# Cross attention: thirteen probability transposes in one run, score steps in runs of 4 and 12, value tiles in blocks of 7 and 6

## The chip, the cores and the metric

One core of one Trainium2 chip runs the whole program. The metric is device time in microseconds (us) for one launch. The time before is the median of three runs.

## The reference, cut to what matters

The program computes one block of a perceiver: cross attention of 32 sequences of 64 rows over a context of 1601 rows each (width 512), then causal self attention with 16 heads, then a two-stage mixture of 64 experts. The change touches cross attention alone:

```python
q = einsum('bsd,ed->bse', layernorm(x), Wq) + bq      # x:   32 x 64 x 512
k = einsum('btd,ed->bte', ctx, Wk) + bk               # ctx: 32 x 1601 x 512
v = einsum('btd,ed->bte', ctx, Wv) + bv
scores = einsum('bse,bte->bst', q, k)
attended = einsum('bst,bte->bse', softmax(scores), v)
x = x + attended
```

The kernel folds `Wq` and `Wk` into one product ahead of time and applies `Wv` after the attention, so that the large loop multiplies queries and probabilities with the raw context.

## The kernel before, in words

**Pairs.** Cross attention works on 16 pairs of sequences (`PAIRS`), so that 2 x 64 query rows fill 128 partitions. For each pair p there are four kinds of work on TensorE:

- `score(pe, p, db)`, 16 steps (`STEPS_S`). Each step multiplies 32 of the 512 features. It needs the context transposed for that step, which VectorE writes into `z`, a ring of 4 slots (`RING`): `blocks` (line 549) makes two transposes for each step, of 7 and of 6 context tiles. VectorE may write a slot again when the score step that read it has finished (line 548). The scores of a pair build up in PSUM banks 0 to 3. A step is 8 calls of `matmul` (line 537), which the trace shows as 16 instructions.
- `transpose_prob(p, g)`, for g = 0 to 3: 4, 4, 4 and 1 transposes of the probabilities (line 676) into PSUM. ScalarE copies each group to `probt` in SBUF (lines 658 and 661).
- `attend(p, j)`, 13 value tiles (`TILES`), each of 4 instructions in the trace (line 686), added up in PSUM bank 6 (`OB`). Each releases part of the context buffer through `s_pv`.
- `transpose_attended(p)`: 4 transposes of the attended rows (line 695) into bank 7 (`AB`).

**Order on TensorE.** The order is written out by hand and shifted by one pair. Iteration p (1 to 15) runs score steps of pair p. Among them it runs the probability transposes of pair p-1, one group ahead of each of the steps 0 to 3, then value tiles 0 to 3 ahead of step 4 and tiles 4 to 6 ahead of step 8. After step 15 come tiles 7 to 12, and then `transpose_attended(p - 2)`. In runs, the score steps are 1, 1, 1, 1, 4 and 8.

**PSUM.** The probability transposes use banks 4 and 5 in turn (`TB + g % 2`), so from the third group on TensorE waits for ScalarE's copy of the group before last (`s_pte`). Value tile j waits for the copy that holds it.

**Between score step 15 and the next transposes.** VectorE takes the maximum of each row (`greatest`, lines 555 to 561), ScalarE then computes the exponentials (`exponentials`, lines 570 to 574, six semaphore increments of `s_exp`), and the first probability transpose of the pair waits for all six. ScalarE's order in an iteration is: `exponentials(p)`, `attended_out(p - 2)` (copies the transposed attended rows out of bank 7, line 644), `attended(p - 1)` (normalises bank 6 into `att`, line 638), four copies of probabilities.

**Loads.** The context lies in 5 slots, two for a pair (7 and 6 tiles). SyncE's queue loads a slot again in two parts, after value tiles 4 and 7 for the slot of the first 7 tiles and after tiles 11 and 13 for the other (lines 597 and 185). It also stores the attended rows (`store_attended`, line 585) and reloads the queries (line 195). The store of pair p-2 stands ahead of the query load in its order.

**The two ends.** Before iteration 1 a preparation stage ends with a small copy on ScalarE (line 408, semaphore `s_re`). TensorE waits for it in iteration 1 after score step 0. After iteration 15 TensorE transposes the last probabilities, does 8 value projections (`values`, line 234, 16 instructions), and then the last pair's 13 value tiles.

Of the kernel before, what the change touches and what calls it, by code (L numbers as in the profile page):

```python
# [27 lines left out]
P = 128  # L28
# [3 lines left out]
QUADS = SEQS // 4  # L32
# [7 lines left out]
FULL = CTX // P  # L40
REST = CTX - FULL * P
RQ = REST // 4
TILES = FULL + 1
# [114 lines left out]
PAIRS = SEQS // 2  # L158
# [73 lines left out]
def values(pe, ps, early, par, c):  # L232

    x = pe.matmul(ps[:, par, :], early.ats[:, c, par::2], early.xwv[:, c, :], start=c == 0, stop=c == DC - 1)  # L234
    if c == DC - 1:
        x.then_inc(early.s_p1, 1)
# [266 lines left out]
def cross(nc, block, sem, zone, area, spare, temp, ps, a, ident, qbias, halves, slots, qs, s_c, s_qs, s_qd, early):  # L503
# [4 lines left out]
    prob = zone(TILES, 4, 32)  # L508
    probt = zone(TILES, P)
# [5 lines left out]
    RAT = FULL * 32  # L515
    WIDTH = (RAT + RQ + 1, RAT + RQ, RAT + RQ, RAT + RQ)
    EXPS = 6
    TB, OB, AB = 4, 6, 7

    s_pad = sem("cr_pad")  # L520
    s_z, s_s, s_pv = sem("cr_z"), sem("cr_s"), early.s_pv
    s_mx, s_top, s_bias = sem("cr_mx"), sem("cr_top"), sem("cr_bias")
    s_exp, s_tot, s_rec = sem("cr_exp"), sem("cr_tot"), sem("cr_rec")
    s_pt, s_pte = sem("cr_pt"), sem("cr_pte")
    s_att, s_at, s_ate = sem("cr_att"), sem("cr_at"), sem("cr_ate")
# [5 lines left out]
    def score(pe, p, db):  # L531
        at = STEPS_S * p + db
        pe.wait_ge(s_z, 2 * at + 2)
        for tb in range(4):
            r = slice(tb * 32, (tb + 1) * 32)
            for b in range(2):
                last = pe.matmul(ps[b * SEQ:(b + 1) * SEQ, tb, 0:WIDTH[tb]],  # L537
                                 qs[p % 2][r, db, b * SEQ:(b + 1) * SEQ], z[r, at % RING, b, 0:WIDTH[tb]],
                                 start=db == 0, stop=db == STEPS_S - 1)
        last.then_inc(s_s, 1)  # L540
# [23 lines left out]
    def exponentials(act, p):  # L564
        act.wait_ge(s_bias, p + 1)
        if p:
            act.wait_ge(s_tot, p)
            act.wait_ge(s_pt, 4 * p)
        for tb in range(4):
            act.activation(prob[:, 0:FULL, tb, :], ps[:, tb, 0:RAT].rearrange("p (j t) -> p j t", t=32), ACT.Exp,  # L570
                           bias=bias[:, 0:1], accum_out=sums[:, tb:tb + 1]).then_inc(s_exp, 1)
        act.activation(prob[:, FULL, :, 0:RQ], ps[:, 0:4, RAT:RAT + RQ], ACT.Exp,
                       bias=bias[:, 0:1], accum_out=sums[:, 4:5]).then_inc(s_exp, 1)
        act.activation(prob[:, FULL, 0, RQ:RQ + 1], ps[:, 0, RAT + RQ:RAT + RQ + 1], ACT.Exp,
                       bias=bias[:, 0:1], accum_out=sums[:, 5:6]).then_inc(s_exp, 1)

    s_re = prepare(nc, block, sem, area, spare, temp, ps, a, ident, qbias, halves, slots, qs, s_c, s_qs, s_qd,
                   s_pad, prob[:, FULL, :, :],
                   {"score": score, "blocks": blocks, "greatest": greatest, "exponentials": exponentials})

    @block.sync
    def _(sp):
        def store_attended(p):
            sp.wait_ge(s_ate, p + 1)
            sp.dma_start(a["at"][p // 2, :, :, p % 2 * P:(p % 2 + 1) * P], att_t).then_inc(s_atd, 16)

        for p in range(PAIRS):
            if p >= 2:
                store_attended(p - 2)
            if p + 2 < PAIRS:  # L590
                sp.wait_ge(s_s, STEPS_S * (p + 1))
                sp.wait_ge(s_qd, 8 * 16 * ((p + 2) // 2 + 1))
                load_queries(sp, a, qs, s_qs, p + 2)
            for k, first in ((2 * p + 5, 0), (2 * p + 6, 7)):
                for part in range(2):
                    if k < 2 * PAIRS:
                        sp.wait_ge(s_pv, TILES * p + min(first + (4, 7)[part], TILES))
                        load_context(sp, a, slots, s_c, k, parts=(part,))
            if p == PAIRS - 3:
                early.load(sp, a)  # L600
                sp.wait_ge(s_pv, TILES * (PAIRS - 2))
                for n in ("swq", "swk", "swv"):
                    sp.dma_start(early.weights[n], a[n].rearrange("(c p) e -> p c e", p=P)).then_inc(early.s_w, 16)
            if p == PAIRS - 2:
                sp.wait_ge(s_pv, TILES * (PAIRS - 2) + 7)
                sp.dma_start(early.weights["swo"], a["swo"].rearrange("(c p) e -> p c e", p=P)).then_inc(early.s_w, 16)
        sp.wait_ge(s_pv, TILES * (PAIRS - 1))
        early.load_own(sp, a)
        store_attended(PAIRS - 2)
        store_attended(PAIRS - 1)  # L610
# [20 lines left out]
    @block.scalar  # L631
    def _(act):
        def attended(p):
            act.wait_ge(s_pv, TILES * (p + 1))
            act.wait_ge(s_rec, p + 1)
            if p:
                act.wait_ge(s_at, p)
            act.activation(att, ps[:, OB, :], ACT.Copy, scale=recip[:, 0:1]).then_inc(s_att, 1)

        def attended_out(p):  # L640
            act.wait_ge(s_at, p + 1)
            if p:
                act.wait_ge(s_atd, 16 * p)
            act.copy(att_t, ps[:, AB, :].rearrange("p (c n) -> p c n", c=DC)).then_inc(s_ate, 1)

        for p in range(PAIRS):
            if p:
                exponentials(act, p)
            if p >= 2:
                attended_out(p - 2)  # L650
            if p:
                attended(p - 1)
            for g in range(4):
                act.wait_ge(s_pt, 4 * p + g + 1)
                if p and g == 0:
                    act.wait_ge(s_pv, TILES * p)
                if g < 3:
                    act.copy(probt[:, 4 * g:4 * g + 4, :], ps[:, TB + g % 2, :].rearrange("p (j n) -> p j n", j=4))\
                       .then_inc(s_pte, 1)
                else:  # L660
                    act.copy(probt[:, FULL, :], ps[:, TB + 1, 0:P]).then_inc(s_pte, 1)
        attended_out(PAIRS - 2)
        attended(PAIRS - 1)
        attended_out(PAIRS - 1)

    @block.tensor
    def _(pe):
        def transpose_prob(p, g):
            if g == 0:
                pe.wait_ge(s_exp, EXPS * (p + 1))  # L670
            n = 4 * p + g
            if n >= 2:
                pe.wait_ge(s_pte, n - 1)
            for j in quarter(g):
                at = (j - 4 * g) * P
                last = pe.transpose(ps[:, TB + g % 2, at:at + P], prob[:, j, :, :].rearrange("p b t -> p (b t)"), ident)  # L676
            last.then_inc(s_pt, 1)

        def attend(p, j):
            if j % 4 == 0:  # L680
                pe.wait_ge(s_pte, 4 * p + j // 4 + 1)
            if j == 0 and p:
                pe.wait_ge(s_att, p)
            slot, jj = (slots[slot_of(2 * p)], j) if j < 7 else (slots[slot_of(2 * p + 1)], j - 7)
            for b in range(2):
                last = pe.matmul(ps[b * SEQ:(b + 1) * SEQ, OB, :], probt[:, j, b * SEQ:(b + 1) * SEQ],  # L686
                                 slot[:, b, jj, :], start=j == 0, stop=j == TILES - 1)
            last.then_inc(s_pv, 1)

        def transpose_attended(p):  # L690
            pe.wait_ge(s_att, p + 1)
            if p:
                pe.wait_ge(s_ate, p)
            for c in range(DC):
                last = pe.transpose(ps[:, AB, c * P:(c + 1) * P], att[:, c * P:(c + 1) * P], ident)
            last.then_inc(s_at, 1)

        for p in range(1, PAIRS):
            pe.wait_ge(s_qs[p % 2], 64 * (p // 2 + 1))
            for db in range(STEPS_S):  # L700
                if p == 1 and db == 1:
                    pe.wait_ge(s_re, 2 * QUADS)
                if db < 4:
                    transpose_prob(p - 1, db)
                if db in (4, 8):
                    for j in ((0, 1, 2, 3) if db == 4 else (4, 5, 6)):
                        attend(p - 1, j)
                score(pe, p, db)
            for j in range(7, TILES):
                attend(p - 1, j)  # L710
            if p >= 2:
                transpose_attended(p - 2)
        for g in range(4):
            transpose_prob(PAIRS - 1, g)
        pe.wait_ge(early.s_xwv, 16)
        pe.wait_ge(early.s_ats, 16)
        for par in range(2):
            for c in range(DC):
                values(pe, ps, early, par, c)
        transpose_attended(PAIRS - 2)  # L720
        for j in range(TILES):
            attend(PAIRS - 1, j)
        transpose_attended(PAIRS - 1)

# [1585 lines left out]
```

## Time and profile before

| what | value |
|---|---|
| median of 3 runs | 1348.16 us (1347.85 to 1349.36) |
| profiled execution, span from first to last instruction | 1344.9 us |
| granted TensorE clock, mean over the span | 0.969 |
| TensorE matmul busy | 1251.8 us, 93% of the span |
| VectorE busy | 797.4 us, 59% |
| ScalarE busy | 439.9 us, 33% |
| period of one pair in cross attention | 26.42 us |

The page's shares are means over three stages with different limits. The change acts only between about 121 us and 540 us of the span. The profile gives no separate launch-to-end time of the profiled execution. Its span lies 3.3 us below the median of the runs, and that part is outside the first and last instruction.

### The profile page before, as it was taken

What the parts mean: (1) busy time and instruction counts of PE and PEld (TensorE: products, weight loads), DVE (VectorE), ACT (ScalarE), POOL (GpSimd) and SP (SyncE); (2) the same over time, 40 slices, a digit from 0 to 9 for tenths busy, and PEclk for the clock granted to TensorE, in tenths of its full rate; (3) what the DMA queues carried; (4) which work ended last, traced back from release to release, by engine and by line L of the source; (5) the groups of instructions that cost most, each with busy time, mean ns of one, the idle gap of its engine ahead of it and who ended that gap; (6) DMA issues with size and microseconds to landing.
All of it is one profiled execution on the core that took longest, in us unless ns stands there. A gap on an engine that the chain in (4) does not pass through costs nothing.

```text
span 1344.9 us, 61468 instructions
## 1 busy us (share of the span) xinstructions
PE 1251.8 (93%) x27944; PEld 813.3 (60%) x27944; DVE 797.4 (59%) x1489; ACT 439.9 (33%) x873; POOL 226.4 (17%) x372
## 2 busy tenths in 40 slices
PE   6999999999999999999999999787898888889886
PEld 4875333333333333676667665666787777779775
DVE  2264777677677763355655655454665746465766
ACT  0332132113112211221222212234554646454564
POOL 0000000000000001121222212114351533212212
PEclk9999999999999999999999999897999998995998
DMA  6686889998998992611011110401311206334012
GB/s 262 203 284 167 294 273 318 293 304 292 313 291 285 316 325 87 113 63 43 19 62 62 62 47 17 109 33 64 125 79 77 117 8 238 134 164 179 28 44 94
DMA packets 68083, 211.52 MB, mean 157 GB/s; under 512 B 14449, under 2 KB 30833, under 8 KB 53521
## 3 DMA queue, kind: packets, MB, share of 16 engines
q1 hardware_dynamic: 67984, 210.16, 46.1%
q8 instruction: 69, 1.13, 0.3%
q14 instruction: 30, 0.24, 0.1%
HBM read 172.37 MB, written 37.75 MB: 156 GB/s over the span
## 4 chain that ended last, share of the span: by engine, by line
PE 77%; DVE 10%; issue 5%; DMA 3%; POOL 2%; ACT 1%; SPq 1%; DVEq 0%; POOLq 0%; ACTq 0%
PE ps L686 14%; PE ps L537 10%; PE ps L1059 8%; PE ps L2142 6%; DVE arena L549 5%; PE ps L2093 4%; PE ps L234 4%; PE ps L1173 4%; PE ps L1080 4%; PE ps L444 3%; PE ps L2071 2%; PE ps L2184 2%; PE ps L676 2%; DVE arena L1823 2%; PE ps L2128 2%
## 5 line engine op out<-in xcount | busy, mean ns | idle before, releaser
L549 DVE STREAM_TRANSPOSE arena<-arena 128x448 f32<-128x448 f32 (+1 forms) x512 | 264.2, 578 | 103.2 <-PE ps L537 85.9
L537 PE MATMUL ps<-arena 32*64 32x400 f32 (+1 forms) x4096 | 202.6, 506 | 0.8
L686 PE MATMUL ps<-arena 128*64 128x512 f32 x832 | 189.1, 598 | 0.0
L537 PEld LDWEIGHTS ps<-arena 32*64 32x64 f32 x4096 | 75.1, 130 | 97.5 <-issue 49.8
L686 PEld LDWEIGHTS ps<-arena 128*64 128x64 f32 x832 | 55.6, 136 | 121.3 <-issue 111.9
L570 ACT ACTIVATE arena<-ps,arena 128x384 f32<-128x384 f32 x64 | 36.3, 581 | 276.4 <-DVE arena L561 276.4
L1059 PE MATMUL ps<-arena 128*128 128x256 f32 x512 | 116.2, 385 | 0.8 <-ACT arena L994 0.8
L1059 PEld LDWEIGHTS ps<-arena 128*128 128x128 f32 x512 | 97.9, 193 | 17.8 <-issue 3.3
L1993 ACT COPY arena<-ps 128x512 f32<-128x512 f32 x128 | 74.9, 586 | 84.5 <-PE ps L2142 58.0
L1823 DVE SCALAR_TENSOR_TENSOR arena<-ps,arena 128x512 f32<-128x512 f32 x64 | 69.9, 1118 | 43.6 <-PE ps L2128 43.3
L2142 PE MATMUL ps<-arena 64*64 64x32 f32 x4096 | 84.1, 236 | 4.3 <-issue 4.0
L859 POOL TENSOR_TENSOR arena<-arena 128x1024 f32<-128x1024 f32 x8 | 18.9, 2368 | 406.5 <-PE ps L686 406.5
L2142 PEld LDWEIGHTS ps<-arena 64*64 64x64 f32 x4096 | 78.0, 153 | 8.2 <-issue 5.3
L2093 PE MATMUL ps<-arena 64*32 64x128 f32 x4096 | 70.3, 277 | 12.2 <-issue 6.3
L2093 PEld LDWEIGHTS ps<-arena 64*32 64x32 f32 x4096 | 59.6, 107 | 23.3 <-issue 18.9
L927 DVE SCALAR_TENSOR_TENSOR arena<-ps,arena 128x512 f32<-128x512 f32 x32 | 20.6, 686 | 81.6 <-PE ps L1070 81.6
L1762 POOL COPY arena<-arena 128x512 f32<-128x512 f32 x64 | 41.7, 656 | 160.8 <-ACT arena L2014 89.0
L2168 PE MATMUL ps<-arena 64*64 64x256 f32 x1024 | 62.0, 394 | 6.1 <-DVE arena L1836 3.5
L234 PE MATMUL ps<-arena 128*128 128x512 f32 x128 | 60.2, 605 | 0.0
L1814 DVE COPY arena<-ps 128x512 f32<-128x512 f32 x64 | 43.6, 687 | 27.5 <-PE ps L2093 27.4
L1080 PE MATMUL ps<-arena 128*64 128x256 f32 x512 | 58.8, 380 | 0.0
L877 POOL TENSOR_TENSOR arena<-arena 128x512 f32<-128x512 f32 x32 | 33.4, 1042 | 150.0 <-DVE arena L944 150.0
(146 smaller groups left out, 1844.4 us busy)
## 6 DMA issues: line engine op xcount, KB each, us to landing
arena<-ctx SPq DMA_DIRECT2D x64, 1024.0 KB
arena<-ctx SPq DMA_DIRECT2D x32, 768.0 KB
arena<-q_n SPq DMA_DIRECT2D x64, 256.0 KB, 11.3
h_n<-arena SPq DMA_DIRECT2D x16, 1024.0 KB, 4.4
arena<-h_n SPq DMA_DIRECT2D x16, 1024.0 KB, 9.3
arena<-x SPq DMA_DIRECT2D x16, 512.0 KB, 4.7
arena<-ctx SPq DMA_DIRECT2D x32, 256.0 KB
x_n<-arena SPq DMA_DIRECT2D x16, 512.0 KB, 3.5
```

What stands on the lines that cost most here:

```text
L234: x = pe.matmul(ps[:, par, :], early.ats[:, c, par::2], early.xwv[:, c, :], start=c == 0, stop=c == DC - 1)
L537: last = pe.matmul(ps[b * SEQ:(b + 1) * SEQ, tb, 0:WIDTH[tb]], qs[p % 2][r, db, b * SEQ:(b + 1) * SEQ], z[r, at % RING, b, 0:WIDTH[tb]], s ...
L549: vec.transpose(z[:, at % RING, :, g * 224:g * 224 + nt * 32].rearrange("p b (j t) -> p b j t", t=32), slots[slot_of(k)][:, :, 0:nt, db * ...
L686: last = pe.matmul(ps[b * SEQ:(b + 1) * SEQ, OB, :], probt[:, j, b * SEQ:(b + 1) * SEQ], slot[:, b, jj, :], start=j == 0, stop=j == TILES - 1)
L1059: last = pe.matmul(ps[:, bank, m % 2 * QROWS:(m % 2 + 1) * QROWS], w[n][:, c, m * P:(m + 1) * P], lnt[:, c, :], start=c == 0, stop=c == DC ...
L1080: last = pe.matmul(ps[e * SEQ:(e + 1) * SEQ, 2 + pair, s2 * 256:(s2 + 1) * 256], lnt[:, c, at:at + SEQ], w["swv"][:, c, :].rearrange("p (m ...
L1173: last = pe.matmul(ps[:, (OUT if more else LAST_OUT) + par, :], aot[:, c, par::2], w["swo"][:, c, :], start=c == 0, stop=c == DC - 1)
L1823: vec.scalar_tensor_tensor(h[:, q, :, at].rearrange("p j g -> p g j"), ps[:, b:b + 2, :].rearrange("p b (g x) -> p (b g) x", x=2 * F1)[:, ...
L1993: act.copy(mid[u].rearrange("p (b x) -> p b x", b=2), ps[:, 2 * u:2 * u + 2, 0:256]).then_inc(s_me, 1)
L2093: last = pe.matmul(ps[c * R:(c + 1) * R, 4 * v + hf, o * P:(o + 1) * P], tab_st[v][r, o, :], x, start=True, stop=True)
L2142: last = pe.matmul(ps[k * F1:(k + 1) * F1, 2 * u + t, g * D1:(g + 1) * D1], st_h[u][rows_t, g * F1:(g + 1) * F1], two(st_a[u])[rows_t, k, ...
L2168: last = pe.matmul(ps[t * E:(t + 1) * E, 2 * (g % 4) + hf, o % 2 * 2 * P:(o % 2 + 1) * 2 * P], tab_dn[v][r, o, :], x, start=True, stop=True)
```

## The change

What it does, part by part:

- The probability transposes of a pair run one after another at the head of an iteration and write four banks: 4, 5, 7 and 6. They no longer wait for ScalarE's copies. Groups 2 and 3 wait instead until banks 7 and 6 have been read (`s_ate`, `s_att`).
- The score steps then run as 0 to 3 and 4 to 15. Between them stand value tiles 0 to 6 and `transpose_attended(p - 2)`. Tiles 7 to 12 stay after step 15.
- The first value tile waits for all four copies of the probabilities.
- In ScalarE's order `attended_out` moves behind the four copies and one pair earlier in index (p-1 in iteration p).
- The wait on `s_re` in iteration 1 moves ahead of the transposes.
- At the end `transpose_attended(PAIRS - 2)` moves from ahead of the last value tiles to between tiles 6 and 7.

```diff
-    TB, OB, AB = 4, 6, 7
+    OB, AB = 6, 7
+    PROB_BANKS = (4, 5, AB, OB)
...
             if p:
                 exponentials(act, p)
-            if p >= 2:
-                attended_out(p - 2)
             if p:
                 attended(p - 1)
             for g in range(4):
                 act.wait_ge(s_pt, 4 * p + g + 1)
-                if p and g == 0:
-                    act.wait_ge(s_pv, TILES * p)
+                bank = PROB_BANKS[g]
...
-        attended_out(PAIRS - 2)
+            if p:
+                attended_out(p - 1)
         attended(PAIRS - 1)
         attended_out(PAIRS - 1)
...
-            n = 4 * p + g
-            if n >= 2:
-                pe.wait_ge(s_pte, n - 1)
+            if PROB_BANKS[g] == AB and p >= 2:
+                pe.wait_ge(s_ate, p - 1)
+            if PROB_BANKS[g] == OB and p:
+                pe.wait_ge(s_att, p)
...
         def attend(p, j):
-            if j % 4 == 0:
-                pe.wait_ge(s_pte, 4 * p + j // 4 + 1)
-            if j == 0 and p:
-                pe.wait_ge(s_att, p)
+            if j == 0:
+                pe.wait_ge(s_pte, 4 * p + 4)
...
         for p in range(1, PAIRS):
             pe.wait_ge(s_qs[p % 2], 64 * (p // 2 + 1))
+            if p == 1:
+                pe.wait_ge(s_re, 2 * QUADS)
+            for g in range(4):
+                transpose_prob(p - 1, g)
             for db in range(STEPS_S):
-                if p == 1 and db == 1:
-                    pe.wait_ge(s_re, 2 * QUADS)
-                if db < 4:
-                    transpose_prob(p - 1, db)
-                if db in (4, 8):
-                    for j in ((0, 1, 2, 3) if db == 4 else (4, 5, 6)):
+                if db == 4:
+                    for j in range(7):
                         attend(p - 1, j)
+                    if p >= 2:
+                        transpose_attended(p - 2)
                 score(pe, p, db)
             for j in range(7, TILES):
                 attend(p - 1, j)
-            if p >= 2:
-                transpose_attended(p - 2)
...
+        for j in range(7):
+            attend(PAIRS - 1, j)
         transpose_attended(PAIRS - 2)
-        for j in range(TILES):
+        for j in range(7, TILES):
             attend(PAIRS - 1, j)
         transpose_attended(PAIRS - 1)
```

## Rows read from the trace of the kernel before

**Rows 1.** Timeline of TensorE, one pair (start us, us, instruction, count).

```profile
305.43 0.66 PE L695 MATMUL ps<-arena 128*128 128x128 f32 x4
305.92 0.60 PE L676 MATMUL ps<-arena 128*128 128x128 f32 x4
306.45 0.93 PE L537 MATMUL ps<-arena 32*64 32x401 f32 x16
...
311.32 3.66 PE L686 MATMUL ps<-arena 128*64 128x512 f32 x16
314.91 2.94 PE L537 MATMUL ps<-arena 32*64 32x401 f32 x64
317.78 2.80 PE L686 MATMUL ps<-arena 128*64 128x512 f32 x12
320.51 6.09 PE L537 MATMUL ps<-arena 32*64 32x401 f32 x128
326.53 5.38 PE L686 MATMUL ps<-arena 128*64 128x512 f32 x24
331.85 0.66 PE L695 MATMUL ps<-arena 128*128 128x128 f32 x4
332.34 0.60 PE L676 MATMUL ps<-arena 128*128 128x128 f32 x4
```

**Rows 2.** Timeline of TensorE, line 695, iterations 2 and 15 (12 lie between).

```profile
173.32 0.66 PE L695 MATMUL ps<-arena 128*128 128x128 f32 x4
...
516.83 0.66 PE L695 MATMUL ps<-arena 128*128 128x128 f32 x4
```

**Rows 3.** Timeline of VectorE and weight loads in the run of eight steps.

```profile
321.55 4.06 DVE L549 STREAM_TRANSPOSE arena<-arena 128x448 f32<-128x448 f32 x8 [1.54 <-PE ps L537]
...
325.67 0.24 PEld L537 LDWEIGHTS ps<-arena 32*64 32x64 f32 x16 [0.75 <-DVE arena L549]
```

**Rows 4.** Timeline from score step 15 to the next transposes, iteration 1 to 2.

```profile
141.64 5.38 PE L686 MATMUL ps<-arena 128*64 128x512 f32 x24
...
147.04 0.23 ACT L574 ACTIVATION_READ_ACCUMULATOR arena<-ps,arena 128x1 f32 x1
147.13 0.71 ACT L638 ACTIVATE arena<-ps,arena 128x512 f32<-128x512 f32 x1
...
147.37 0.63 PE L676 MATMUL ps<-arena 128*128 128x128 f32 x4 [0.35 <-issue]
...
148.03 0.59 ACT L658 COPY arena<-ps 128x512 f32<-128x512 f32 x1 [0.19 <-PE ps L676]
```

**Rows 5.** Timeline, start of iteration 1.

```profile
121.00 0.64 PE L676 MATMUL ps<-arena 128*128 128x128 f32 x4
121.55 0.26 ACT L408 ACTIVATE arena<-ps,arena 128x2 f32<-128x2 f32 x1
```

**Rows 6.** Timeline, end of iteration 15.

```profile
517.32 1.04 PE L676 MATMUL ps<-arena 128*128 128x128 f32 x8
...
519.88 7.04 PE L234 MATMUL ps<-arena 128*128 128x512 f32 x16
```

**Rows 7.** Waits of VectorE, 120 to 540 us (total, times, longest).

```profile
DVE arena L549 <- PE ps L537: 78.9, 47, 3.6
DVE arena L549 <- DMA arena<-ctx: 17.0, 13, 2.4
```

**Rows 8.** Loads: timeline of one pair; DMA issues by line (last number: median us to landing).

```profile
323.55 3.07 SPq L189 DMA_DIRECT2D arena<-ctx  x5
...
at_n<-arena SPq DMA_DIRECT2D x16, 256.0 KB, 10.7
```

**Rows 9.** Windows: length, busy us (count) of PE, PEld, DVE, ACT, POOL; clock, DMA share, GB/s.

```profile
320.50:326.53 6.03, 5.98 (x130) 2.46 (x128) 4.06 (x8) 0.00 (x0) 0.00 (x0) 1.00 0.99 374
...
910.00:915.00 5.00, 1.92 (x9) 1.95 (x10) 0.00 (x0) 0.00 (x0) 0.00 (x0) 0.57 0.01 3
915.00:920.00 5.00, 5.00 (x25) 5.00 (x24) 0.00 (x0) 0.00 (x0) 0.00 (x0) 0.50 0.02 3
```

More of the change, by code:

```diff
@@ L654, in _ @@
                 act.wait_ge(s_pt, 4 * p + g + 1)
-                if p and g == 0:
-                    act.wait_ge(s_pv, TILES * p)
+                bank = PROB_BANKS[g]
                 if g < 3:
-                    act.copy(probt[:, 4 * g:4 * g + 4, :], ps[:, TB + g % 2, :].rearrange("p (j n) -> p j n", j=4))\
+                    act.copy(probt[:, 4 * g:4 * g + 4, :], ps[:, bank, :].rearrange("p (j n) -> p j n", j=4))\
                        .then_inc(s_pte, 1)
                 else:
-                    act.copy(probt[:, FULL, :], ps[:, TB + 1, 0:P]).then_inc(s_pte, 1)
-        attended_out(PAIRS - 2)
+                    act.copy(probt[:, FULL, :], ps[:, bank, 0:P]).then_inc(s_pte, 1)
+            if p:
+                attended_out(p - 1)
         attended(PAIRS - 1)
@@ L670, in transpose_prob @@
                 pe.wait_ge(s_exp, EXPS * (p + 1))
-            n = 4 * p + g
-            if n >= 2:
-                pe.wait_ge(s_pte, n - 1)
+            if PROB_BANKS[g] == AB and p >= 2:
+                pe.wait_ge(s_ate, p - 1)
+            if PROB_BANKS[g] == OB and p:
+                pe.wait_ge(s_att, p)
             for j in quarter(g):
                 at = (j - 4 * g) * P
-                last = pe.transpose(ps[:, TB + g % 2, at:at + P], prob[:, j, :, :].rearrange("p b t -> p (b t)"), ident)
+                last = pe.transpose(ps[:, PROB_BANKS[g], at:at + P], prob[:, j, :, :].rearrange("p b t -> p (b t)"), ident)
             last.then_inc(s_pt, 1)
         def attend(p, j):
-            if j % 4 == 0:
-                pe.wait_ge(s_pte, 4 * p + j // 4 + 1)
-            if j == 0 and p:
-                pe.wait_ge(s_att, p)
+            if j == 0:
+                pe.wait_ge(s_pte, 4 * p + 4)
             slot, jj = (slots[slot_of(2 * p)], j) if j < 7 else (slots[slot_of(2 * p + 1)], j - 7)
```

## The prediction

> **What bounds the kernel now.** I read the page first, then the timeline of TensorE over two pairs, then the same stretch with VectorE, ScalarE and the load queue, then the waits. The page gives TensorE 93% matmul busy, but its matmuls are pipelined, so I go by start-to-start times. In cross attention the groups of TensorE follow one another and the pair repeats: 305.92 to 332.34 is 26.42 us [rows 1], and the thirteen periods from 173.32 to 516.83 give 26.42 each [rows 2]. Four score steps in a run take 314.91 to 317.78, 2.87 us. Eight take 320.51 to 326.53, 6.02 us [rows 1]. Two runs of four would be 5.74. The difference is the first thing to see: the ring holds four steps, and beyond that VectorE sets the pace. It starts 1.04 us after the run does, does 8 transposes in 4.06 us (0.508 each, 1.015 a step), and TensorE's last step follows at 325.67, 0.06 us after VectorE's end [rows 3]. So the chain here is TensorE, then VectorE, then TensorE.
>
> The second thing is the boundary. Score step 15 ends and the tiles start at 326.53. The tiles last until 331.85, and the next probability transposes start at 332.34, 5.81 us after 326.53 [rows 1]. Between iterations 1 and 2, where no `transpose_attended` fills the gap, they start at 147.37, 5.73 us after 141.64, right behind the last exponential (147.27) and not at the tiles' end (141.64 + 5.32 = 146.96) [rows 4]. So the row maxima and the exponentials set this start, and `transpose_attended` lies in a gap of 0.41 us that TensorE has anyway.
>
> **The change part by part.** I write T for the start of the tiles behind score step 15, and add up one iteration from T to the next T. The prices are start-to-start times that hold the cost of going to the next kind.
>
> *Boundary.* Nothing on the chain from VectorE through ScalarE moves ahead of the exponentials. The transposes start at T + 5.73 as in iteration 2 [rows 4]. Before it was 5.81, so 0.08 is gained.
>
> *Thirteen transposes in a run.* Eight in a run take 1.04 where four take 0.60, so one more is 0.11 [rows 1, 6]. Four up to the next score step are 0.53, so thirteen are 0.53 + 9 x 0.11 = 1.52. Then four steps, 2.87. Together 4.39. Before, the same work took 305.92 to 311.32, 5.40 [rows 1]. This gains 1.01: changes of kind fall away, and ScalarE's copies no longer stand between. The copies must be done before tile 0, at T + 5.73 + 4.39 = T + 10.1. ScalarE normalises first (0.71 from 147.13, so until T + 6.2), waits for the first group (T + 5.73 + 0.66) and then makes four copies of 0.59 at most [rows 1, 4], up to T + 8.8. The cover is the four score steps, with 1.3 us to spare; without them tile 0 would stand 1 to 2.4 us later. Group 3 writes bank 6 at T + 7.05 (12 x 0.11 on), after that normalisation, so its new wait costs nothing. Bank 7 is read out in the middle of the iteration before and costs nothing either.
>
> *Ring.* VectorE makes steps 0 to 3 from T + 2.6 on (reductions first) and is done before T + 9.2 even with its longest wait for a load, 2.4 us [rows 7]. Steps 4 to 7 are made under the tiles. The ring is full when the long run starts.
>
> *Seven tiles.* 16 instructions take 3.59, 12 take 2.73 [rows 1], and one change of kind (0.15: 3.59 less 16 x 0.215, the 0.215 from the difference of the two) falls away: 3.59 + 2.73 - 0.15 = 6.17. This gains 0.15.
>
> *`transpose_attended`.* In the middle of the iteration it covers no gap. It costs what four transposes up to a score step cost, 0.53 [rows 1]. This is the only place where its cost becomes visible.
>
> *Twelve steps.* Four are in the ring, and eight are left for VectorE: 1.04 + 16 x 0.508 + 0.06 + the last step up to T (325.67 to 326.53, 0.86) = 10.08 [rows 1, 3]. Before, runs of 4 and 8 took 2.87 + 6.02 = 8.89, since VectorE refilled the ring under tiles 4 to 6. This loses 1.19. If the last ring slots were free sooner it could not help: TensorE never has a step ready in this run that VectorE has not just made. The lower bound is a run paced by TensorE alone: three runs of four less two changes of kind, 3 x 2.87 - 2 x 0.15 = 8.3. I take the 10.08, since the rows show that pace.
>
> *Sum.* 5.73 + 1.52 + 2.87 + 6.17 + 0.53 + 10.08 = 26.90, against 26.42: +0.48 in each of 14 iterations (2 to 15), +6.7. The check by differences: -0.08 - 1.01 - 0.15 + 0.53 + 1.19 = +0.48.
>
> *Iteration 1.* The wait for `s_re` now stands ahead of the transposes. ScalarE's copy ends at 121.81 [rows 5], so they start near 121.95 instead of 121.00: +0.95. The shorter first part gives back 1.01. There is no `transpose_attended`, so tiles and long run make 1.19 - 0.15 = +1.04. Together +1.0.
>
> *End.* After iteration 15 the transposes start 0.08 earlier and take 1.52 where 517.32 to 519.88, 2.56, were spent with two waits for copies [rows 6]: -1.1. The four attended transposes only change place there.
>
> *Loads and queue.* On SyncE's queue the store no longer waits for ScalarE, and the query loads behind it go out some 0.5 us sooner. The second part of the g = 1 slot is now asked for at T - 10.6, before at T - 6; its last requests ended at 326.62 [rows 8]. VectorE's waits for loads (17.0 us in 13 pairs [rows 7]) should shrink or vanish, but they were under the tiles, so I count nothing. ScalarE's `attended_out` now waits for a store asked for at about T + 6, which lands 10.7 later [rows 8], at T + 17, about when its input is ready. Behind it stand the next exponentials, needed at T + 29. Slack 11, cost nothing.
>
> Total: +1.0 + 6.7 - 1.1 = +6.6. On the profiled span 1344.9 to 1351.5. With the 3.3 that lies outside it, and no change to the later stages except the shift, 1348.2 + 6.6 = **1354.8 us**.
>
> **Rivals.**
> *A. The long run is not paced by VectorE* (ends faster). Then twelve steps are 8.3, the pair 25.12, and 15 pairs gain 1.3 each, the ends nothing: about 1329. For it: VectorE idles 78.9 us on TensorE in this stage [rows 7], so in total it has time. Against: those waits come when the ring is full, and 325.67 stands 0.06 behind VectorE in every period. It decides from the point where VectorE's share of the run is 0.48 us shorter, that is 0.06 of 1.015 in each of 8 steps. Chance 0.05.
>
> *B. The pieces cancel* (no measurable change). It needs 0.3 us a pair that I do not see, say a score run that restarts sooner behind `transpose_attended`, or thirteen transposes that overlap the steps. Time 1346 to 1350.8. Chance 0.10.
>
> *C. A new wait in the middle*: copies late for tile 0, or loads in one burst that reach VectorE late. With 1 us a pair: 1354.8 + 15 = 1370. For it: the margin of the copies is only 1.3. Against: each of its parts has a row. Chance 0.06.
>
> *D. TensorE's clock falls in the paced run.* In the run of eight, with the last steps paced by VectorE, the granted clock is 1.00, the level of 2.4 GHz. At 915 to 920 us, after 5 us in which TensorE was busy for 1.92, it is 0.50, that of 1.2 GHz [rows 9]. In the new run TensorE waits about 0.33 us a step (1.015 less 8.3 / 12). At the lower level the run would be 16.6, +6.5 us a pair: 1452. Chance 0.02. The Trainium skill, "TensorE: Matmul & The Clock Gate", section "A second HAM failure mode: psum-queue depth-cycling", says that a kernel which cycles through PSUM banks and leaves small idle gaps between groups of matmuls can swing between the two clock levels; this would speak against four banks and a paced run. By that rule the time would be rival D's. The trace does not agree so far: the paced part it has runs at 1.00.
>
> **How the numbers follow.** My own case, slower by 6.6, has 0.77. Its bounds: the boundary 5.73 or 5.81 (1.1 us over 14), the transposes 1.43 to 1.60 (2.5 us; 13 x 0.11, or 0.60 + 9 x 0.11), attended transposes 0.44 (4 x 0.11) to 0.60 (2.2 us), the later stages 1 us. This makes 1352 to 1358. A change under 0.2% (2.7 us) cannot be told from none. For 8 in 10 I take 1351 to 1359, which reaches a little toward B and C. Faster 0.06 (A and the far end of B), same 0.10, slower 0.84.
>
> **What would show it.** In the new timeline: thirteen transposes of line 676 in about 1.5 us with no ScalarE wait among them, 4.4 us from their start to tile 0; 28 tile instructions in 6.2; line 695 behind them; then 192 score instructions in 10.1 with VectorE unbroken over 16 transposes, ending just ahead of the last step; and T to first transpose 5.7. The distance of two starts of line 695 should be 26.9. I am wrong if the long run takes under 9.5, if the distance is 26.4 or less, or if a wait stands ahead of tile 0.

## The result, and where the time went

The changed kernel takes 1383.73 us (median, 1376.12 to 1389.08, 4 runs) against 1348.01: a ratio of 1.0262, with a 95% interval of 1.0232 to 1.0291. That is slower, as forecast, but by 35.7 us where 6.6 were forecast, and outside the range. The profiled execution has a span of 1387.2 us against 1344.9, 42.3 more; it was the slowest of the four (1389.08 us), so its surplus is larger than that of the medians. Here 1.9 us lie outside the first and last instruction, so the 3.3 us of the section on the time before were only in part that; the rest is scatter between executions. The ratios here leave out runs more than 1.5% above the fastest of their kernel, which are one run of the kernel before, of 6326.19 us and unexplained, and four of the ten of e11.

First the part that was changed. One pair on TensorE in the timeline of the changed kernel (columns as in [rows 1]):

```profile
305.96 5.38 PE L684 MATMUL ps<-arena 128*64 128x512 f32 x24
311.73 1.61 PE L676 MATMUL ps<-arena 128*128 128x128 f32 x13 [0.39 <-ACT arena L575]
313.27 2.94 PE L538 MATMUL ps<-arena 32*64 32x401 f32 x64
316.14 6.25 PE L684 MATMUL ps<-arena 128*64 128x512 f32 x28
322.31 0.66 PE L693 MATMUL ps<-arena 128*128 128x128 f32 x4
322.90 10.03 PE L538 MATMUL ps<-arena 32*64 32x401 f32 x192
332.86 5.38 PE L684 MATMUL ps<-arena 128*64 128x512 f32 x24
```

Start to start these are 5.77, 1.54, 2.87, 6.17, 0.59 and 9.96, together 26.90. The prediction had 5.73, 1.52, 2.87, 6.17, 0.53 and 10.08, together 26.90. VectorE in the long run, and ScalarE ahead of tile 0 of the next pair:

```profile
323.94 8.01 DVE L550 STREAM_TRANSPOSE arena<-arena 128x448 f32<-128x448 f32 x16 [5.32 <-PE ps L538]
```

```profile
338.35 0.71 ACT L639 ACTIVATE arena<-ps,arena 128x512 f32<-128x512 f32 x1
339.30 1.56 ACT L656 COPY arena<-ps 128x512 f32<-128x512 f32 x3 [0.23 <-PE ps L676]
340.73 0.30 ACT L659 COPY arena<-ps 128x128 f32<-128x128 f32 x1
```

Sixteen transposes without a break, starting 1.04 us behind the run and ending at 331.95, 0.91 ahead of the next tiles: VectorE paces the run, as in [rows 3]. The copies end at 341.03, and tile 0 of that pair starts at 343.05.

The head and the end of cross attention:

```profile
122.69 0.51 PE L459 MATMUL ps<-arena 128*128 128x1 f32 x4
123.98 1.61 PE L676 MATMUL ps<-arena 128*128 128x128 f32 x13 [0.78 <-issue]
...
527.56 1.64 PE L676 MATMUL ps<-arena 128*128 128x128 f32 x13 [0.29 <-ACT arena L575]
529.04 7.04 PE L234 MATMUL ps<-arena 128*128 128x512 f32 x16
```

Line 234 starts at 529.04, 9.2 us later than in [rows 6]. Of these 2.0 were lost ahead of the changed code: the last matmul of line 459 starts at 122.9, before at 120.9. (Over the kernels below it starts anywhere from 119.9 to 126.7, so that is scatter.) The changed part itself costs 7.1 up to here. Behind it, up to the first start of line 1050, the order with `transpose_attended` between the last tiles costs 0.3 more (550.15 - 529.04 = 21.11 where 540.66 - 519.88 = 20.78 was).

The rest is far away from the change. I take the down steps of the mixture from the first to the last start of line 2184 (`second_dn`), a line that is the same in both. Before they ran from 1155.4 to 1334.8, 179.4 us; now from 1162.9 to 1377.0, 214.1 us. So they start 7.5 later (the stages between had given 1.7 of the 9.2 back) and take 34.7 more, and with 0.1 behind them that is the whole 42.3. Windows over this stretch (columns as in [rows 9]), of the kernel before:

```profile
1155.00:1209.00 54.00, 45.52 (x1929) 40.12 (x1931) 32.24 (x57) 25.91 (x40) 11.73 (x18) 0.97 0.44 177
1209.00:1249.00 40.00, 38.95 (x1464) 35.69 (x1460) 17.65 (x32) 16.92 (x30) 10.78 (x18) 0.53 0.41 158
1249.00:1335.00 86.00, 74.32 (x3552) 64.74 (x3544) 62.40 (x85) 52.62 (x81) 23.26 (x34) 1.00 0.13 49
```

and of the changed kernel:

```profile
1163.00:1223.00 60.00, 46.54 (x1934) 40.66 (x1932) 32.37 (x57) 27.44 (x42) 12.40 (x19) 0.97 0.41 160
1223.00:1267.00 44.00, 38.03 (x1420) 35.20 (x1422) 17.62 (x31) 14.42 (x26) 10.08 (x16) 0.50 0.37 145
1267.00:1333.00 66.00, 56.56 (x2168) 47.16 (x2160) 45.27 (x55) 39.29 (x56) 13.89 (x20) 0.98 0.09 33
1333.00:1377.00 44.00, 36.66 (x1405) 34.36 (x1408) 17.35 (x30) 14.42 (x26) 8.59 (x14) 0.52 0.13 49
```

Before, one window of 40 us has a granted clock near 0.5 (the level of 1.2 GHz, not 2.4). Now there are two of 44. The timeline shows what TensorE did just ahead of the first of them:

```profile
1215.38 1.10 PE L2168 MATMUL ps<-arena 64*64 64x256 f32 x16
1216.27 1.11 PE L2142 MATMUL ps<-arena 64*64 64x32 f32 x64
1222.85 0.29 PE L2184 MATMUL ps<-arena 128*32 128x32 f32 x2 [5.46 <-issue]
1225.22 0.65 PE L2184 MATMUL ps<-arena 128*32 128x32 f32 x30 [2.09 <-issue]
```

TensorE stands still for 5.46 us, runs two matmuls, and stands still for 2.09 more, in the middle of a group of 32. Nothing that the profile shows released it ("issue"): no semaphore, no transfer of data. This is where the loop over groups of rows jumps back to the head of the down steps. The loop has four groups, so there are three such jumps. The third, at 1335.72, stalls in the same way (5.30 and 1.97 us). The second, at 1286.36, does not: the wait there is 0.81 us and is put down to GpSimd. In the kernel before no jump stalls. At the first of them the wait is 0.76 us, put down to ScalarE, and a wait for issue of 0.68 us stands ahead of the jump, 20 matmuls into the last group. The clock falls there too:

```profile
1207.19 0.52 PE L2142 MATMUL ps<-arena 64*64 64x32 f32 x20
1208.39 0.89 PE L2142 MATMUL ps<-arena 64*64 64x32 f32 x44 [0.68 <-issue]
1210.04 0.46 PE L2184 MATMUL ps<-arena 128*32 128x32 f32 x32 [0.76 <-ACT arena L1993]
```

The view of the DMA queues points to a cause, with packets, MB and share of queue 8, which carries instructions. Over the down steps before, and then now:

```profile
q8 instruction: 7, 0.11, 0.3%
```

```profile
q8 instruction: 21, 0.34, 0.8%
```

Seven loads of 16 KB have become 21. Three of them start inside the first stall, in the window 1217 to 1225:

```profile
q8 instruction: 3, 0.05, 4.0%
```

The changed kernel has 16 wait instructions less on TensorE than the one before (counted in the programs as built, where several waits of the text can become one instruction: 148 against 164) and 15 less on ScalarE. All that TensorE runs later stands 16 instructions earlier in its instruction stream.

### The profile page after: what moved, and what is told of

Read it like the earlier page. It is cut to its first block, busy times and chain, and to the rows that moved or that the text cites. A ratio compares the mean times of both kernels' runs of the same rounds, so it can differ in the third digit from the quotient of the medians.

```text
span 1387.2 us, 61437 instructions
## 1 busy us (share of the span) xinstructions
PE 1269.1 (91%) x27944; PEld 831.9 (60%) x27944; DVE 794.9 (57%) x1489; ACT 437.1 (32%) x873; POOL 225.7 (16%) x372
## 4 chain that ended last, share of the span: by engine, by line
PE 67%; DVE 17%; issue 6%; ACT 4%; DMA 3%; POOL 2%; SPq 1%; DVEq 0%; POOLq 0%; ACTq 0%
DVE arena L550 9%; PE ps L1059 8%; PE ps L684 8%; PE ps L2142 6%; PE ps L538 6%; PE ps L2093 4%; PE ps L234 4%; PE ps L1173 4%; PE ps L1080 4%; PE ps L444 3%; PE ps L2184 3%; DVE arena L556 2%; PE ps L2071 2%; ACT arena L571 2%; DVE arena L1823 2%
## 5 line engine op out<-in xcount | busy, mean ns | idle before, releaser
L550 DVE STREAM_TRANSPOSE arena<-arena 128x448 f32<-128x448 f32 (+1 forms) x512 | 261.2, 575 | 113.6 <-PE ps L538 103.6
L684 PE MATMUL ps<-arena 128*64 128x512 f32 x832 | 186.1, 596 | 0.0
L1059 PE MATMUL ps<-arena 128*128 128x256 f32 x512 | 115.2, 383 | 0.8 <-ACT arena L994 0.8
L2142 PE MATMUL ps<-arena 64*64 64x32 f32 x4096 | 95.8, 252 | 7.2 <-issue 7.0
L2142 PEld LDWEIGHTS ps<-arena 64*64 64x64 f32 x4096 | 89.1, 173 | 11.9 <-issue 8.6
L2093 PEld LDWEIGHTS ps<-arena 64*32 64x32 f32 x4096 | 59.3, 107 | 23.7 <-issue 18.8
L1849 DVE COPY arena<-ps 128x128 f32<-128x128 f32 x64 | 18.6, 291 | 86.7 <-PE ps L2184 86.4
L927 DVE SCALAR_TENSOR_TENSOR arena<-ps,arena 128x512 f32<-128x512 f32 x32 | 20.6, 686 | 81.2 <-PE ps L1070 81.2
L2184 PE MATMUL ps<-arena 128*32 128x32 f32 x2048 | 40.0, 221 | 25.1 <-issue 23.9
L444 PE MATMUL ps<-arena 128*128 128x256 f32 x256 | 59.5, 385 | 0.0
```

Source lines behind the costliest of these rows:

```text
L444: last = pe.matmul(ps[:, QB + h, m % 2 * QROWS:(m % 2 + 1) * QROWS], wqk[:, c, m * P:(m + 1) * P], lnt[n][:, c, :], start=c == 0, stop=c = ...
L550: vec.transpose(z[:, at % RING, :, g * 224:g * 224 + nt * 32].rearrange("p b (j t) -> p b j t", t=32), slots[slot_of(k)][:, :, 0:nt, db * ...
L1059: last = pe.matmul(ps[:, bank, m % 2 * QROWS:(m % 2 + 1) * QROWS], w[n][:, c, m * P:(m + 1) * P], lnt[:, c, :], start=c == 0, stop=c == DC ...
L2093: last = pe.matmul(ps[c * R:(c + 1) * R, 4 * v + hf, o * P:(o + 1) * P], tab_st[v][r, o, :], x, start=True, stop=True)
L2142: last = pe.matmul(ps[k * F1:(k + 1) * F1, 2 * u + t, g * D1:(g + 1) * D1], st_h[u][rows_t, g * F1:(g + 1) * F1], two(st_a[u])[rows_t, k, ...
L2184: last = pe.matmul(ps[c * R:(c + 1) * R, 4 + u, (2 * t + r) * D1:(2 * t + r + 1) * D1], mid[u][:, at:at + D1], two(st_b[u])[:, t, g * D1:( ...
```

## The experiments

**Theory L**: the place of TensorE's code. It supposes that a loop head has moved to just ahead of a boundary of the blocks in which instructions are loaded. The jump back would then wait for more blocks, and TensorE's idle time would bring the lower clock with it. **Rival S**: the later stages only start later, and meet loads or the clock in a worse phase. Other rivals: ScalarE's code in place of TensorE's, and the new order itself.

**e1: 16 empty instructions on TensorE.**

```diff
         for j in range(7, TILES):
             attend(PAIRS - 1, j)
+        for _ in range(16):
+            apart(pe, SPARE)
         transpose_attended(PAIRS - 1)
```

> The changed kernel with 16 empty instructions (increments of a semaphore that nobody reads) on TensorE ahead of its last transpose_attended. The program of the changed kernel has 16 wait instructions less on TensorE than the one before, so this puts the loops of the mixture stage back at the place in TensorE's instruction stream that they had before. Theory L (place of TensorE's code): the down steps of the mixture take some 190 us again in place of 224, no waits of 5 us ahead of line 2184, the q8 instruction packets of that stage near 8 and not 23; time 1355 to 1358 (before plus the 8 of cross attention). Rival S (the later stages are slow because they start 8 us later, in another phase of clock or loads): 1376 to 1389 as the changed kernel.

Measured: 1354.57 us (10 runs), ratio 1.0054 (1.0039 to 1.007). The down steps take 177.7 us with 7 instruction packets, although they start at 1165.2, later than in either kernel. Rival S falls. The 16 instructions cost nothing that can be seen: the last transposes follow the tiles at the same distance as without them. The line of queue 8 over e1's down steps:

```profile
q8 instruction: 7, 0.11, 0.3%
```

**e2: 15 empty instructions on ScalarE.**

```diff
+        for _ in range(15):
+            act.sem_inc(SPARE[nc.vector.engine], 1)
         attended(PAIRS - 1)
```

> The changed kernel with 15 empty instructions on ScalarE (it has 15 wait instructions less on that engine), TensorE untouched. Theory L for TensorE: no help, 1376 to 1389. Rival, ScalarE's code is the one that is fetched late: 1355 to 1358.

Measured: 1385.4 us, ratio 1.0306 (1.0241 to 1.0371). The down steps take 212.3 us, with 15 packets. It is not ScalarE's code. TensorE's program is that of the changed kernel, and yet another jump stalls: the second (5.29 and 2.27 us), not the first and third.

**e3: the kernel before with 16 waits less on TensorE.**

```diff
         def transpose_prob(p, g):
...
-            if n >= 2:
+            if n >= 2 and g:
                 pe.wait_ge(s_pte, n - 1)
...
         def attend(p, j):
...
-            if j == 0 and p:
-                pe.wait_ge(s_att, p)
```

> The kernel before, same order of all work, with 16 waits left out on TensorE that other waits already imply (s_pte of group 0, s_att at value tile 0). Cross attention is unchanged. Theory L: the same loss as the changed kernel's outside cross attention, 20 to 33 us, so 1368 to 1382, with the waits of 5 us ahead of line 2184. Rival S and every theory that blames the new order: 1348, no change.

The 30 waits that this leaves out of the text are 16 instructions in the program as built.

Measured: 1391.8 us, ratio 1.0328 (1.0295 to 1.036). Cross attention keeps its 26.42 us a pair. The down steps take 225.7 us, 46.3 more than before, with 21 packets. The stall stands in the same place, again at the first and the third jump (line 2182 here is line 2184 there):

```profile
1209.79 1.11 PE L2140 MATMUL ps<-arena 64*64 64x32 f32 x64
1216.01 0.29 PE L2182 MATMUL ps<-arena 128*32 128x32 f32 x2 [5.10 <-issue]
1218.40 0.65 PE L2182 MATMUL ps<-arena 128*32 128x32 f32 x30 [2.10 <-issue]
```

Again two matmuls, then thirty. Nothing about the order of the work was changed here. The loss was larger than I expected, while the waits for issue are not longer than in the changed kernel (26.8 us against 29.6). The clock is lower: 0.70 in the mean over these steps, 0.78 in the changed kernel and 0.89 before. So the loss outside cross attention, the some 28 us of the expectations, needs no new order of the work.

**e4: only the run of thirteen transposes** (steps 4, 4 and 8; tiles 4, 3 and 6; `transpose_attended` behind tile 12; 16 empty instructions as in e1).

```diff
                 if db == 4:
-                    for j in range(7):
+                    for j in (0, 1, 2, 3):
+                        attend(p - 1, j)
+                if db == 8:
+                    for j in (4, 5, 6):
                         attend(p - 1, j)
-                    if p >= 2:
-                        transpose_attended(p - 2)
                 score(pe, p, db)
             for j in range(7, TILES):
                 attend(p - 1, j)
+            if p >= 2:
+                transpose_attended(p - 2)
```

ScalarE's `attended_out(p - 2)` goes back behind the exponentials.

> Only the run of thirteen transposes over four banks is kept. Score steps run as 4, 4 and 8 with tiles 0 to 3, 4 to 6 and 7 to 12 as before, and transpose_attended stays behind tile 12. 16 empty instructions keep TensorE's code where it was. Per pair: 5.81 + 1.52 + up to 0.2 (bank 6 is normalised late) + 2.87 + 3.59 + 2.87 + 2.73 + 6.02 = 25.4 to 25.6 against 26.42: -0.8 to -1.0 a pair, in all 1333 to 1337. If the transposes in a run were not what gains: 1348. If theory L is wrong: 1360 or more.

Measured: 1331.97 us, ratio 0.9908 (0.9873 to 0.9943), faster than both kernels, by 0.9% against the one before. One pair:

```profile
345.10 5.38 PE L685 MATMUL ps<-arena 128*64 128x512 f32 x24
350.42 0.66 PE L694 MATMUL ps<-arena 128*128 128x128 f32 x4
350.91 1.76 PE L677 MATMUL ps<-arena 128*128 128x128 f32 x13
352.60 2.94 PE L538 MATMUL ps<-arena 32*64 32x401 f32 x64
...
370.69 0.65 PE L685 MATMUL ps<-arena 128*64 128x512 f32 x2
```

The pair is 25.59 us. The transposes take 1.69 with the wait for bank 6 (line 677 waits 14 times for line 639, 2.3 us in all), where the four groups among score steps made 5.40 - 2.87 = 2.53.

**e5: runs of 4, 4, 4 and 4** (tiles 3, 2, 2 and 6, else as e4).

```diff
                 if db == 4:
-                    for j in (0, 1, 2, 3):
+                    for j in (0, 1, 2):
                         attend(p - 1, j)
                 if db == 8:
-                    for j in (4, 5, 6):
+                    for j in (3, 4):
+                        attend(p - 1, j)
+                if db == 12:
+                    for j in (5, 6):
                         attend(p - 1, j)
```

> As e4, with the score steps in four runs of 4 and tiles in blocks of 3, 2, 2 and 6, so that VectorE can refill the ring ahead of every run. If VectorE's pace in long runs is what costs: 5.81 + 1.7 + 4 x 2.87 + 7 tiles in three blocks (28 x 0.215 + 3 x 0.15 = 6.5) = 25.5 a pair against 25.6 of e4, so 1 to 2 us faster than e4, 1330 to 1331. If it is not: the one more change of kind costs, 1 to 4 us slower than e4. TensorE's code stays where it was.

Measured: 1334.66 us, ratio 0.9901 (0.9871 to 0.993). The pair is 25.47 us (325.81 to 351.28 in the timeline), 0.12 less than in e4 as expected. The whole doesn't show it: the intervals of e4 and e5 overlap, and in e5's profile the stage ahead of iteration 1 ends at 126.7 against 119.9. Whether e5 is the faster order stays open.

**e6: 8 empty instructions on TensorE** in the changed kernel (the loop of e1 with 8).

> The changed kernel with 8 empty instructions on TensorE in place of the 16 of e1. Theory L with a boundary in the instruction stream close behind the head of the down steps' loop: either all of the 28 us comes back (1355, 7 instruction packets in that stage) or none (1376 to 1389, 15 or more). A time in the middle would speak for a cost that grows with distance.

Measured: 1382.5 us (2 runs), ratio 1.0258 (1.0207 to 1.0309), down steps 202.0 us, 15 packets. None of it comes back. Here the second jump stalls, and the two matmuls that ran between the two waits are gone (line 2186 here is line 2184 there):

```profile
1279.54 0.66 PE L2186 MATMUL ps<-arena 128*32 128x32 f32 x32 [7.87 <-issue]
```

That fits a boundary that has come nearer to the loop head.

**e7: the blocks of the change alone**, tiles 0 to 6 ahead of step 4 and steps 4 and 12, against e4.

```diff
                 if db == 4:
-                    for j in (0, 1, 2, 3):
-                        attend(p - 1, j)
-                if db == 8:
-                    for j in (4, 5, 6):
+                    for j in (0, 1, 2, 3, 4, 5, 6):
                         attend(p - 1, j)
```

> The block sizes of the change alone against e4: tiles 0 to 6 in one block, score steps 4 and 12, transpose_attended behind tile 12, code where it was. My sum: 5.81 + 0.2 + 1.52 + 2.87 + 6.17 + 10.08 = 26.65 a pair, so +1.05 a pair on e4, in all 1347 to 1351. If the long run is not paced by VectorE (rival A): 1310 to 1325. The rest up to e1 (0.26 a pair, 4 us) is transpose_attended in the middle.

Measured: 1348.38 us (10 runs), ratio 1.0001 (0.9986 to 1.0015). Its pair:

```profile
329.39 5.38 PE L685 MATMUL ps<-arena 128*64 128x512 f32 x24
334.71 0.66 PE L694 MATMUL ps<-arena 128*128 128x128 f32 x4
335.20 1.76 PE L677 MATMUL ps<-arena 128*128 128x128 f32 x13
336.89 2.94 PE L538 MATMUL ps<-arena 32*64 32x401 f32 x64
339.77 6.25 PE L685 MATMUL ps<-arena 128*64 128x512 f32 x28
345.94 10.03 PE L538 MATMUL ps<-arena 32*64 32x401 f32 x192
355.90 1.51 PE L685 MATMUL ps<-arena 128*64 128x512 f32 x6
```

From 329.39 to 355.90 it is 26.51. So the two block sizes give back 0.92 us a pair of what the run of transposes gains: the run of twelve costs 1.07, the block of seven tiles gains 0.15. Fifteen pairs make 13.8; the medians of e7 and e4 lie 16.4 apart. e1's pair is 26.91 (306.43 to 333.34), 0.40 more, which is what `transpose_attended` in the middle costs in the net: 0.59 for itself, less 0.04 at the boundary and 0.15 of the wait for bank 6, which e1 has not. Fourteen pairs make 5.6; e1 lies 6.2 above e7.

**e8: e5 with 80 empty instructions** in place of 16.

> As e5 with 80 empty instructions on TensorE in place of 16. Theory L with fixed blocks: other loops and jumps now cross a boundary, or none. If the place does not matter beyond the loop head: as e5 within 4 us. If a larger shift moves another loop over a boundary: 10 us or more slower, with more instruction packets.

Measured: 1368.85 us, ratio 1.0163 (1.0111 to 1.0215). The down steps are the fastest of all kernels, 171.4 us at a clock of 0.98. But 82 instruction packets were loaded ahead of them, where every kernel above has 62, and TensorE waited elsewhere. Its waits from 505 us to the down steps:

```profile
PE ps L2102 <- issue: 20.9, 9, 5.8
...
PE ps L694 <- issue: 7.9, 1, 7.9
```

Line 2102 is the gather of the up stage, one loop earlier. In e5, which differs by the 64 instructions alone, it waited 6.6 us. The second row stands right behind the 80 empty instructions. These two make 22 of the 35 us by which the down steps start later than in e5; the other 13 are not put down to lines here. Ahead of the down steps the clock is at 0.50 for 78.5 us in all, in e5 for 34.1.

**e9, e10 and e11: e4 with 0, 12 and 32 empty instructions** (the loop of e1 with these numbers).

> e4 without its 16 empty instructions: the order that gains some 14 us, with TensorE's code at the place where the changed kernel has it. Theory L: 1332 + 28 = 1356 to 1368, with 15 or more instruction packets in the down steps. A better order would be measured as a loss. Otherwise: 1332.

Measured: 1363.9 us, ratio 1.0139 (1.0099 to 1.018), down steps 201.7 us, 15 packets. An order that gains 15.6 us with the code in its old place reads as a loss of 1.4%.

> e4 with 12 empty instructions in place of 16. 8 were not enough (e6), 16 are (e1). Either 1332 or 1356 to 1368, no time between; it says on which side of 12 the boundary lies.

Measured: 1335.82 us (2 runs), ratio 0.9916 (0.9896 to 0.9937), down steps 179.5 us, 7 packets. The time turns between 8 and 12 instructions; if theory L holds, the boundary lies that far on.

> e4 with 32 empty instructions. With 80 the down steps took 171 us at 7 packets in place of 178, but 20 packets more were loaded ahead of them and the stretch from line 234's last start to the down steps grew. If 32 lies on the good side of both boundaries: 1325 to 1332; if it is past the other one: 1360 or more.

Measured: 1348.2 us (10 runs), ratio 0.9964 (0.9929 to 0.9999). Its runs scatter from 1329.95 to 1358.95, where those of before stay within 4.3 us. The profiled one has 7 packets and 179.7 us in the down steps, and 74 packets ahead of them. The median lies between the two outcomes expected, so the run settles neither. That the slower runs among them had a stall, which would make one place good in one run and bad in the next, is not shown: the one trace is of an execution of 1339.37 us.

## Why the prediction was wrong

**What held.** Every term of the pair came within 0.12 us. That the sum is exact (26.90) is luck: the long run was 0.12 shorter, and the other terms 0.12 longer. The pacing by VectorE, the visible cost of `transpose_attended` (0.59 for 0.53), the hidden copies and the late `s_re` wait (123.98 - 122.69 = 1.29 where the first transposes stood 0.38 behind before, +0.9 for 0.95) are all in the rows. Cross attention cost 7.1 up to line 234 where 6.6 was the sum, with one wait for issue of 0.49 in the thirteenth iteration that no other had, and 0.3 at the end for the attended transposes, which the prediction counted as nothing. With the code back at its place, the kernel takes 1354.57 against the 1354.8 predicted (e1). The change forecast there was right; a match to 0.2 us is again luck, since the down steps of e1's profile are 1.7 us shorter than those of before and medians of the kernel before range from 1346.8 to 1348.2 between sessions.

**The step that failed** is the one in the total: "no change to the later stages except the shift". The down steps took 34.7 us more. Their code is the same, but its place in TensorE's instruction stream was not. I priced the 16 waits that went away by their time alone. They are also 16 instructions that stand ahead of every later loop. e1 and e3 show this from both sides: put back, the loss outside cross attention is gone; taken out of the kernel before, with the order of all work kept, a loss of 44 us appears. With 0 (the changed kernel, e9) and 8 empty instructions (e6) the down steps are slow, with 12 (e10) and 16 (e1, e4) they are fast, whichever of the two orders of work they follow. So the place in the stream is shown as the cause; that it acts through blocks and their boundary is the reading that fits the loads inside the stall, and no run moved a boundary by itself.

**How the 34.7 are made up.** Waits of TensorE for issue over the down steps (lines 2184, 2142 and 2168 in the view of waits) went from 13.1 to 29.6 us, +16.5. The time at the lower clock, summed from the clock records of the traces, went from 41.0 to 93.4 us, +52.4. The same three numbers can be read for every kernel here (waits for issue at all lines of TensorE; the last column names the jumps with a stall of 5 us or more):

| kernel | down steps, us | waits for issue, us | at 0.50, us | packets | stalled jumps |
|---|---|---|---|---|---|
| before | 179.4 | 13.1 | 41.0 | 7 | none |
| changed | 214.1 | 29.6 | 93.4 | 21 | 1, 3 |
| e1 | 177.7 | 14.1 | 34.1 | 7 | none |
| e2 | 212.3 | 17.6 | 116.1 | 15 | 2 |
| e3 | 225.7 | 26.8 | 134.7 | 21 | 1, 3 |
| e6 | 202.0 | 22.0 | 81.9 | 15 | 2 |
| e8 | 171.4 | 17.1 | 6.8 | 7 | none |
| e9 | 201.7 | 20.6 | 78.5 | 15 | 2 |

The other five (e4, e5, e7, e10, e11) are like before or e1: 7 packets and no stall. In all thirteen the time of the down steps is 151.7 us, plus the waits, plus 0.36 us for each us at the lower clock, within 1.5 us. This is a fit to the traces, and an estimate. By it the 52.4 us cost 18.8, and with the 16.5 of waits they make 35.3 of the 34.7 measured. So the loss is about half waits and half clock.

That a stall brings the lower clock is in the order of events: at each of the seven stalled jumps in these traces (the last column) the clock is at 1.00 when the wait begins and falls to 0.50 before it ends. It is not the only way to the lower clock. The kernel before falls to it behind waits of 0.68 and 0.76 us, and e2 has more of it than the changed kernel with only one stall. In the changed kernel a pair of second and first products takes 2.4 to 2.7 us start to start at 0.50, where it takes 1.4 to 1.8 at 1.00 in the kernel before, unless a wait falls into it.

**The rivals.** A fell: the run took 9.96. B and C fell as well: no pieces cancelled, and no new wait stood in the middle. D fell too: every window of 30 us in cross attention has a granted clock of 1.00, with the waits of up to 0.75 us that the long run leaves. The lower level came in the mixture, most of it behind stalls of 5 us, and for no reason that D names. The rule of the Trainium skill that I set beside D is not borne out for the four banks and the paced run.

**What could have been seen.** The Trainium skill, "Runtime: NRT & Kernel Launch", section "Instruction fetch mechanics", says that instructions are fetched in blocks of 16 KiB and that a taken branch to a block outside the current window waits for a fetch. The trace agrees: 0.34 MB in 21 packets are 16 KB each, and the stall stands at a backward jump. The page gives no price. Here it is 5.46 + 2.09 us for one jump, the clock behind it not counted. The kernel before had the mark already, waits for issue at line 2184, 9.0 us in its down steps. I read the waits only for cross attention.

**What stays open.** Part of the difference between 15 and 21 packets is in the table: 21 go with stalls at the first and third jump, 15 with one at the second, so each stalled jump goes with 7 or 8 more loads. Why these jumps and not the others, when the changed kernel and e2 have the same TensorE program, stays open. So does what lowers the clock where no jump stalls, and why e11 scatters.

## What to carry to other kernels

A change that adds or removes even a few instructions, waits too, moves every later loop of that engine in its instruction stream, and a loop may stand where that costs: here 8 empty instructions were too few and 12 were enough. Before such a change is blamed or praised, compare a stage that it doesn't touch, look at the waits for issue and at the instruction queue there, and run it once more with as many empty instructions as it took away. Here that turned a loss of 2.6% into one of 0.5%, and for a better order a loss of 1.4% into a gain of 0.9%.

A run of producer and consumer longer than the ring pays the producer's pace for each step beyond the ring. Grouping work of one kind gains only as long as no such run grows: here 0.83 us a pair came from the transposes, and 1.07 went back with the run of twelve.

## What the runs showed of the hardware

- One backward jump of TensorE waited 5.46 + 2.09 us in the changed kernel, 5.10 + 2.10 in e3 and 7.87 in one piece in e6. In the kernel before, where its target stood 16 instructions further on, it waited 0.76 us, put down to ScalarE. In no slow kernel did all three jumps stall.
- After such a stall the granted clock was 0.50 in a window of 44 us, in which TensorE was busy for 38.0 us with small matmuls. Over the thirteen profiles a us at 0.50 cost the down steps some 0.36 us (an estimate, from the fit above).
- 16 empty semaphore increments on TensorE hid behind matmuls and a ScalarE wait. Behind 80 of them stood a wait of 7.9 us, about 0.1 us each if nothing else is in it.
